# Key tiles of the exponentials added on GpSimd ahead of one 512-column sum on TensorE

## The reference

```python
L_y = einsum('bhqd,bhkd->bhqk', q, k_y) * scale
agg = sum(exp(clip(L_y, -15.0, 15.0)) * mask, axis=-1) + EPS
L = einsum('bhqd,bhkd->bhqk', q, k) * scale
r = log(abs(L) + EPS) - log(agg + EPS)
w = softplus(r) * mask
A = w / (sum(w, axis=-1) + EPS)
out = einsum('bhqk,bhkd->bhqd', A, v)
```

## Time and profile before

| | us |
|---|---|
| median of 3 runs | 1381.5 |
| lowest and highest | 1379.47, 1383.17 |
| the profiled execution | 1381.93 |
| its span in the profile | 1380.1 |
| PE busy, share of the span | 1271.8, 92% |
| DVE busy | 720.5, 52% |
| ACT busy | 616.0, 45% |
| POOL busy | 118.2, 9% |
| PE matmuls of `sum_exps` (L677, `e_ring`) | 89.7 |
| POOL masks (L287) | 78.5 |

### The profile page before, as it was taken

How to read it: one execution, slowest core, us unless ns; L and a number is a source line. 1 busy time by engine, 2 the same in 40 slices (tenths; PEclk the granted TensorE clock), 3 DMA queues, 4 the chain that set the end, 5 groups by cost and what they waited for, 6 DMA issues and landing times.

```text
span 1380.1 us, 22940 instructions
## 1 busy us (share of the span) xinstructions
PE 1271.8 (92%) x8310; PEld 813.9 (59%) x8310; DVE 720.5 (52%) x1223; ACT 616.0 (45%) x810; POOL 118.2 (9%) x140
## 2 busy tenths in 40 slices
PE   5988999999999999985499999999999999999996
PEld 1433444444344444432388788787887878878785
DVE  2556767676777768576143533535235353343523
ACT  3566767667676766654132412323123241332411
POOL 1111111211112111110000000000000000000000
PEclk9999999999999999998699999999999999999998
DMA  2002222222221321000460000000000000000000
GB/s 74 16 17 69 94 62 92 76 91 76 79 102 47 106 76 54 1 32 16 170 251 16 31 0 15 30 15 30 0 15 30 15 30 0 15 30 15 30 0 16
DMA packets 31944, 66.89 MB, mean 48 GB/s; under 512 B 2849, under 2 KB 8609, under 8 KB 31905
## 3 DMA queue, kind: packets, MB, share of 16 engines
q1 hardware_dynamic: 31904, 66.35, 14.2%
HBM read 46.42 MB, written 19.92 MB: 48 GB/s over the span
## 4 chain that ended last, share of the span: by engine, by line
issue 51%; POOL 0%; DVE 0%; POOLq 0%; DVEq 0%
POOL f_rstd L813 0%; DVE f_res L820 0%; POOLq L913 0%; DVEq L825 0%; POOL f_minus_half L911 0%; POOLq L83 0%
## 5 line engine op out<-in xcount | busy, mean ns | idle before, releaser
L939 ACT ACTIVATE f_h_full<-f_layer_bank,f_scales 128x512 f32<-128x512 f32 x128 | 88.0, 687 | 354.7 <-PE f_layer_bank L1053 354.6
L502 DVE TENSOR_TENSOR w_ring<-score_banks,keep 128x1024 int32<-128x1024 int32 (+1 forms) x192 | 191.7, 1040 | 56.9 <-PE score_banks L651 56.9
L353 ACT ACTIVATE e_ring<-score_banks 128x1024 f32<-128x1024 f32 (+1 forms) x192 | 158.8, 879 | 136.9 <-PE score_banks L651 136.6
L1053 PE MATMUL f_layer_bank<-f_ha_hi,f_w_all 128*128 128x512 f32 x512 | 204.2, 399 | 2.7 <-DVE f_h_full L981 2.3
L1053 PE MATMUL f_layer_bank<-f_ha_lo,f_w_all 128*128 128x512 f32 x512 | 202.6, 396 | 0.0
L1053 PE MATMUL f_layer_bank<-f_hb_hi,f_w_all 128*128 128x512 f32 x512 | 202.5, 396 | 0.0
L1053 PE MATMUL f_layer_bank<-f_hb_lo,f_w_all 128*128 128x512 f32 x512 | 202.3, 395 | 0.0
L493 DVE TENSOR_SCALAR e_ring<-e_ring 128x2048 f32<-128x2048 f32 (+1 forms) x96 | 100.4, 1046 | 118.0 <-ACT e_ring L353 117.9
L360 ACT ACTIVATE w_ring<-w_ring 128x2048 f32<-128x2048 f32 (+1 forms) x96 | 156.7, 1632 | 7.2 <-DVE w_ring L502 7.0
L287 POOL TENSOR_SCALAR_AFFINE_SELECT e_ring<-e_ring 128x512 f32<-128x512 f32 (+1 forms) x96 | 78.5, 818 | 475.8 <-DVE e_ring L493 475.0
L651 PE MATMUL score_banks<-q,ky 32*128 32x512 f32 (+3 forms) x1024 | 98.1, 475 | 22.4 <-DVE w_ring L502 19.3
(11 more groups left out here) (101 smaller groups left out, 1534.7 us busy)
## 6 DMA issues: line engine op xcount, KB each, us to landing
piece<-in_wf SPq DMA_DIRECT2D x44, 256.0 KB, 2.8
wf_copy<-piece SPq DMA_DIRECT2D x44, 256.0 KB, 2.9
f_w_all<-wf_copy SPq DMA_DIRECT2D x2, 4096.0 KB, 24.8
f_x_turn<-x SPq DMA_DIRECT2D x9, 512.0 KB, 3.3
xq<-in_xt SPq DMA_DIRECT2D x8, 512.0 KB, 3.3
xv<-in_xt SPq DMA_DIRECT2D x8, 512.0 KB, 3.5
res<-in_xn SPq DMA_DIRECT2D x8, 512.0 KB, 4.1
x<-res SPq DMA_DIRECT2D x8, 512.0 KB, 2.8
```

Source lines behind the costliest of these rows:

```text
L353: nc.scalar.activation(e_ring[:, t % RING, 2 * i:2 * i + 2, 0:cols], pair_banks(y_pair(t, i), cols), ACT.Exp).then_inc(exp_done, 1)
L502: nc.vector.tensor_tensor(w_ring[:, t % RING, 2 * i:2 * i + 2, 0:cols].bitcast(I32), pair_banks(w_pair(t, i), cols).bitcast(I32), keep[:, ...
L939: nc.scalar.activation(h_full[m % 2][:], f_bank[m % RING][:], ACT.Gelu, scale=scales[:, 1 + layer, m:m + 1]).then_inc(gelu_done, 1)
L1053: mm = nc.tensor.matmul(out, left.bitcast(dt), right.bitcast(dt), start=first and n == 0, stop=last and n == 1)
```

## The change

The exponentials of a quad's first chunk now go into `e_sum`, which has a place for each of the unit's two quads, those of the other two chunks into `e_more[1]` and `e_more[2]` (`exps_of`). Behind its mask, GpSimd adds each key tile of the second and third chunk onto the queries of `e_sum` that see it (`add_keys`, three instructions per quad). TensorE sums the keys of a quad only once, over 512 columns, in the beat behind the quad's last (`sum_exps`, now in beats 3 and 0 only), and waits there for the third add. `sum_weights` opens and closes the accumulation of the weights by itself. `c_spread` is written by ScalarE (`spread_make`, beat 1, behind `logs`) and no longer by VectorE.

```diff
-        e_ring = sb("e_ring", [P, RING, QUAD, T])
+        e_sum = sb("e_sum", [P, 2, QUAD, T])
+        e_more = [None, sb("e_more1", [P, QUAD, T]), sb("e_more2", [P, QUAD, T // 2])]
...
+        def exps_of(t):
+
+            return e_sum[:, t // CHUNKS, :, :] if t % CHUNKS == 0 else e_more[t % CHUNKS][:]
...
+            def add_keys(k, t):
+
+                added = 3 * quad_of(k, t) + (0, 0, 2)[t % CHUNKS]
+                reach(pool, e_masked, y_beat(k, t) + 1)
+                for n, (at, j) in enumerate(CHUNK_TILES[t % CHUNKS]):
+                    reach(pool, e_added, added + n)
+                    queries = e_sum[:, t // CHUNKS, :, P * j:T]
+                    nc.gpsimd.tensor_tensor(queries, queries, exps_of(t)[:, :, at:at + T - P * j], ALU.add).then_inc(e_added, 1)
...
                     if y:
                         mask_e(k, t)
+                    if y and t % CHUNKS:
+                        add_keys(k, t)
...
-                reach(act, e_summed, y_beat(k, t) - RING + 1)
+                if t % CHUNKS == 0:
+                    reach(act, e_summed, quad_of(k, t) - 1)
+                else:
+                    reach(act, e_added, 3 * quad_of(k, t) + t % CHUNKS - 2)
...
+            def spread_make(v):
+
+                reach(act, cols_step, 2 * v.index + 2)
+                reach(act, spread_ready, v.index)
+                nc.scalar.copy(c_spread[:], c_cols[:, :, 0:HU].unsqueeze(3).to_broadcast([P, TI, HU, HD])).then_inc(c_spread_made, 1)
...
+                    if t == 1 and before[0]:
+                        spread_make(k.shift(-1))
...
                 nc.vector.reciprocal(c_cols[:], agg_eps[:]).then_inc(cols_step, 1)
-                reach(dve, cols_step, start + 2)
-                nc.vector.tensor_copy(c_spread[:], c_cols[:, :, 0:HU].unsqueeze(3).to_broadcast([P, TI, HU, HD])).then_inc(cols_step, 2)
...
+            def sum_exps(k, g, alone):
+
+                reach(pe, e_added, 3 * (2 * k.index + g + 1))
+                if alone:
+                    reach(pe, acc_copied, 2 * k.index + g)
+                for r in range(QUAD):
+                    mm = nc.tensor.matmul(acc[lanes(r), :], sum_exp[:], e_sum[:, g, r, :], start=alone, stop=alone)
+                mm.then_inc(e_summed, 1)
...
-                    if sums[0]:
-                        sum_exps(*last, not sums[1])
+                    if t % CHUNKS == 0 and sums[0]:
+                        sum_exps(last[0], last[1] // CHUNKS, not sums[1])
```

53 lines of the change are left out of this document (25 added, 28 removed).

## The result

The changed kernel takes 1427.2 us (median; 1425.69 to 1428.97), the kernel before 1382.0 in the same comparison: 1.033 times as long, 95% interval 1.031 to 1.035. The forecast was 1383 us, and its range, 1372 to 1411, does not hold the time. TensorE did lose work, as meant.

A forecast was written before the change was run, and what follows sets the result against it. Waits between engines, followed beat by beat, bound the loop rather than TensorE's busy time alone (36.74 of 38.01 us). Profiled 1381.9 us, +0.5 for the phase (-2.3, +4.8, -2), +1 for the adds: 1383 us, range 1372 to 1411.

The forecast's parts named there:

- The first two units: Units with no or few weights: nothing waits for the removed sums, so they give 0 to 6.2 us; taken as -2.
- the adds on GpSimd: GpSimd reading while VectorE works: 0 to 2 us in all, the 2 being clip of beat 2 late in half 0.
- Beats 0 and 3, +0.42: The 512-column sum ahead of the weights' scores replaces a 256-column one, uncovered: +0.42 us per beat, both halves.
- Beats 1, 2, 4, 5: Sums removed: beat 1 -0.24 us, beat 2 0, beat 4 0, beat 5 about -1.00 in half 0, 0 in half 1.
- The spread factors: Copy moved to ScalarE in beat 1: clip 0.16 us earlier at most, ScalarE cost 0 to 0.06, taken as 0.
- Rival 3: GpSimd's adds late at TensorE's sum in beat 3, 40% longer: 1396 us; 0.06 together with a compare held in one half.
- The adds, 5.8 us a quad: Three GpSimd adds priced in proportion to base_v's row: 0.97, 2.90 and 1.94 us, 5.8 in 19 us.
- GpSimd is the one that pays: From the rstd row (1.88 us against 1.01 alone): when GpSimd and VectorE overlap GpSimd slows, which costs nothing here.
- rival 1: Beat 1: GpSimd's second add holds VectorE's compare, next scores 2.3 to 2.7 us late in 11 units; 1410 us, chance 0.27.
- S+14.2: When TensorE reaches beat 3's sum in half 0, counted from S, the start of beat 1's scores.
- the spare 0.9 us: Half 0, beat 3: the third add ends about S+13.3, 0.9 us before TensorE's sum; more in half 1 and beat 0.
- the toss: Beat 1: whether the second add (S+6.85) or the compare (S+6.83) starts first, called a coin's toss.

The follow-up runs named there:

- e4: Kernel before, with the sums of exponentials in beats 0 and 3 moved behind the weights' scores; 1371.5 us, 0.9929 times the kernel before.
- e15: Changed kernel with all key adds cut to one column a head, plus four all-zero matmuls in beat 5 of half-1 units; 1385.9 us.
- e2: Changed kernel with the spread copy of the factors back on VectorE; 1429.4 us, 1.0343 times the kernel before.
- e3: Kernel before, plus the same GpSimd adds on two scratch tiles that nobody waits for; 1409.3 us, 1.019 times the kernel before.
- e13: Changed kernel with each quad's first two adds (beats 1 and 4) cut to one column a head, the third whole; 1394.7 us.
- e11: Changed kernel with each quad's third add (beats 2 and 5) cut to one column a head, the other two whole; 1409.8 us.
- e7: Changed kernel with the long adds cut into pieces of 128 columns a head, six adds a quad; 1425.5 us.
- e8: Changed kernel with the sums of exponentials of beats 0 and 3 behind the weights' scores; 1404.9 us, 1.0167 times the kernel before.
- e1: Changed kernel with all key adds cut to one column a head; 1391.3 us, 1.0067 times the kernel before.
- e10: Changed kernel with all key adds cut to one column a head and the sums of beats 0 and 3 behind the weights' scores; 1366.0 us.

## Why the prediction failed, step by step

Two terms of the sum failed. The first two units were put at -2 us and came to +22.75; the adds on GpSimd were put at +1 and lengthen a pair of loop units by 2.0 of the 2.4 us that it lost. Both go back to two readings: that the adds are done when TensorE wants them, and that GpSimd pays where it meets VectorE.

**Beats 0 and 3, +0.42.** Right: 6.52 to 6.95 and 6.04 to 6.47 with tiny adds. e4 shows the same chain from the other side.

**Beats 1, 2, 4, 5.** Beat 1 gave 0.17 for 0.24, beat 2 nothing in half 0 and 0.11 in half 1, and in half 0 beat 4 gave 0.26 where the forecast said that the gain is lost at once, and beat 5 gave 0.65 instead of 1.00. Together half 0 gained 0.21 for 0.39, half 1 lost 0.58 for 0.60, which is so close by some luck: the 0.11 was not in the forecast. Without the adds and with the clock up (e15) this is the forecast's loop: +1.6 us over 11 units, forecast +0.7.

**The spread factors.** Right, as far as e2 can tell.

**The first two units, -2.** With tiny adds it is -2.4. But this is the step that failed most: +22.75. The sum of the adds and the spare time were worked out for a unit of the loop, where TensorE comes to the sum of beat 3 at S+14.2, 8.4 us after the adds begin, and carried over to the units without weights, where it comes 3.4 us after (34.43 against 31.04). It waited 5.8, 3.3 and 5.4 us. Rival 3 was right here, and I had placed it in the loop alone. The waits are not all: the spare adds of e3, for which nobody waits, make the third unit begin 4.6 us later than before. With all adds tiny it begins at 72.70 us, with the third add whole at 73.18 (e13), with the other two whole at 85.69 (e11), and with all three whole at 97.90: the third alone costs 0.5 us, the first two alone 13.0, and all three 25.2.

**The adds, 5.8 us a quad.** 7.2: the second took 3.58 us where base_v's row gave 2.90. The estimate from the GPSIMD Engine Reference of the Trainium skill ("Performance versus the Vector engine"), 3.37 us, was nearer. In the loop the spare 0.9 us nearly covered it (0.12 us late in half 1).

**"GpSimd is the one that pays."** Wrong, and it carried the whole choice between forecast and rival 1. The row behind it was a GpSimd operation of four columns. The prediction says that the compare lay over it, but not that the compare was there first. From the kernel before (timeline):

```profile
368.74 0.69 DVE L565 SCALAR_TENSOR_TENSOR piece_hi<-piece,piece_hi 128x512 fp32r<-128x512 f32 x1
...
599.62 1.39 POOL L813 TENSOR_TENSOR rstd<-var_eps,minus_half 128x4 f32<-128x4 f32 x1 [4.01 <-DVE var_eps L807]
...
599.74 1.23 DVE L493 TENSOR_SCALAR e_ring<-e_ring 128x2048 f32<-128x2048 f32 x1
```

The compare was running when the `rstd` of 368.81 started, so that row was no case of GpSimd first. The one of 599.62 is: no VectorE operation on SBUF alone was running, `clip` came 0.12 us behind and took its usual time, and `rstd` took 1.39 us for 1.01 (and the same in the trace of every run). So for this small operation the forecast's reading stands; for the adds it does not, and why the two differ stays open. An add held `clip`, the compare, `att_den` and the norm's scaling whenever one of them came up behind it. Operations with an operand in PSUM (`absolute`, `qc`, `res`) keep their times, and so does, in the one row in which it met an add, the reciprocal `att_inv`, SBUF to SBUF (172.41 us in e7, 0.55 us as always). SBUF — State Buffer of the Trainium skill ("Who interferes with whom") says that the one that starts first keeps the shared pair for its whole instruction; the trace agrees for the adds (2.43, 2.79 and 2.33 us, and 1.23 in e7's pieces) and for `base_sum` behind `clip` (1.28 us in e8), but not for the `rstd` of 599.62.

**Rival 1** had the mechanism and not the place. The compare of beat 1 came up between the two adds and lost 0.1 us, as the toss allowed. I asked only about the operation with two inputs in SBUF, and not about the next in the queue, `clip` of beat 2, for which I had given 2 us at most, nor about the norm's scaling and `att_den`, which the adds of beats 4 and 5 meet. These cost 0.88 and 1.03 us in half 0 (e13, e11) and nothing in half 1, where these beats are no longer than with tiny adds (6.95, and 5.71 for 5.69): 1.9 of the 2.4 us that a pair of units lost. The other 0.5 is the order (+0.37) and the 0.12 of beat 3 in half 1.

**The clock.** The sum has no term for it. In most loop units of the changed kernel it stands at 1.00, but not in the first ones (0.57 from 70 to 90 us), and not with tiny adds: in e1 it fell behind a wait of 1.84 us, and with that wait filled it did not (e15). What share of the 22.75 us is waiting (14.5 by the profile), held operations and clock was not parted by a run, but for the 4.6 us of e3. The clock of the first 97.90 us is 0.86 in the mean, so by an estimate from that it can account for 13.7 us at most; in the kernel before it is 1.00 over the first 75.15.

## What to carry over

Before work is put on GpSimd, list every VectorE instruction that comes up while it runs, not only the one that looks exposed, and ask of each whether all its operands are in SBUF and what queues behind it; an operation of 64 columns can take 2.33 us instead of 0.25. Read, too, what else was running in the row that a price is taken from. Work out the spare time of a moved step for the first and last units as well as for the loop, and price the step from an instruction with the same operands. And a beat table (start to start of one matmul group) tells in one look which part of a change did what: most of the gain to be had was not in the sums that left TensorE (5.5 us, e10 beside e4) but in the place of the sums of beats 0 and 3 (10.5 us, e4).

## What the runs showed of the hardware

- A VectorE operation held by a GpSimd add is recorded as long (2.33 us for 64 columns), not as waiting; VectorE looks busier (810 for 720 us) without having more to do.
- It goes the other way too: a GpSimd operation that starts while such a VectorE operation runs is long (`base_sum` 1.28 for 0.29 us, e8).
- The same two-input adds take 0.68, 1.76 and 1.21 us on VectorE for 512, 1536 and 1024 columns, and 1.28, 3.58 and 2.38 on GpSimd.
- Less work on TensorE can bring its clock down: with the sums gone it fell to 1.2 GHz behind a wait of 1.84 us in four of the loop's five units of half 1 (e1); with 1.06 us of idle matmuls in that wait it did not in any of the loop.
